# Where eight float32r operands of a mixture-of-experts stage lie in SBUF

## What is computed

```python
x = layernorm(x + ssm(x))
x = layernorm(x + int8_expert(x, fside, ctx))
# mixture: h = x as [1024, 256]; gate_up_proj [8, 352, 256]; down_proj [8, 256, 176]; router_w [8, 256]
probs = softmax(h @ router_w.T); vals, idx = top_k(probs, 2); vals /= vals.sum(-1)
combine[token, idx] = vals
for gup, dp, cw in experts:
    gate, up = split(h @ gup.T, 2)
    out += cw[:, None] * (silu(gate) * up @ dp.T)
x = layernorm(x + out)
```

## The kernel before

| tensors | start modulo 512 |
|---|---|
| `x2_hi`, `x2_lo` (moving in gate_up) | 352 |
| `gu_hi`, `gu_lo` (stationary in gate_up) | 224 |
| `hid_hi`, `hid_lo` (stationary in down) | 416 |
| `dp_hi`, `dp_lo` (moving in down) | 352 |
| `ident`, `ones` | 352 |
| `tokens`, `u_feat`, `w_feat`, `cw1`, `cw2`, `diag` | 128 |
| `gu_raw`; `xq`, `wq`, `scale_rows` | 160; 32 |

## Time and profile before

### The profile page before, as it was taken

One profiled execution on the slowest core, in us unless ns is written; L12 is line 12 of the kernel. 1 busy time (PEld: TensorE's weight loads), 2 busy tenths in 40 slices (PEclk: granted clock), 3 DMA queues, 4 the chain that ended last, 5 costly groups with the idle time before them and its releaser, 6 DMA issues.

```text
span 160.5 us, 3397 instructions
## 1 busy us (share of the span) xinstructions
PE 146.4 (91%) x1158; PEld 139.7 (87%) x1158; DVE 111.2 (69%) x385; ACT 86.9 (54%) x187; POOL 81.0 (50%) x131
## 2 busy tenths in 40 slices
PE   6778579987899999999999999999999999999980
PEld 6566457876799998999999999999999999999970
DVE  3999957989888979699827886966735652444252
ACT  6431496489876787735466866355554404335210
POOL 5613499486966468622119564224835213337421
PEclk9999987999999999999999999999999999999998
DMA  3899990000000374000246100017430025620001
GB/s 104 263 383 422 354 325 22 0 0 0 6 0 4 87 150 121 7 0 4 66 154 146 35 0 33 6 30 158 135 111 0 0 55 122 159 62 6 33 0 65
DMA packets 13313, 14.55 MB, mean 91 GB/s; under 512 B 1744, under 2 KB 13040, under 8 KB 13040
## 3 DMA queue, kind: packets, MB, share of 16 engines
q1 hardware_dynamic: 13296, 14.34, 29.7%
HBM read 13.25 MB, written 1.08 MB: 89 GB/s over the span
## 4 chain that ended last, share of the span: by engine, by line
PE 75%; DMA 7%; DVE 6%; ACT 3%; SPq 3%; issue 2%; POOL 1%; POOLq 0%; ACTq 0%
PE ps_gu L351 13%; PE ps_gu L356 13%; PE ps_gu L352 13%; DMA gu_raw<-in_guT 7%; PE ps_out L372 6%; PE ps_out L376 6%; PE ps_out L373 6%; PE ps_ab L385 3%; PE ps_ab L390 2%; PE ps_s L385 2%; ACT gu_hi L775 1%; PE ps_gu L407 1%; PE ps_ab L486 1%; SPq L255 1%; PE ps_tr L322 1%
## 5 line engine op out<-in xcount | busy, mean ns | idle before, releaser
L351 PE MATMUL ps_gu<-x_hi,gu_hi 128*128 128x256 f32 x176 | 46.5, 286 | 0.0
L352 PE MATMUL ps_gu<-x_hi,gu_lo 128*128 128x256 f32 x176 | 45.6, 281 | 0.0
L1185 POOL TENSOR_TENSOR gu_raw<-gu_raw 128x512 f32<-128x512 f32 (+1 forms) x24 | 28.5, 1196 | 22.2 <-DVE gu_raw L1575 14.8
L356 PE MATMUL ps_gu<-x_lo,gu_hi 128*128 128x256 f32 x176 | 35.2, 282 | 0.0
L351 PEld LDWEIGHTS ps_gu<-x_hi,gu_hi 128*128 128x128 f32 x176 | 33.1, 188 | 0.1
L352 PEld LDWEIGHTS ps_gu<-x_hi,gu_lo 128*128 128x128 f32 x176 | 33.2, 188 | 0.0
L356 PEld LDWEIGHTS ps_gu<-x_lo,gu_hi 128*128 128x128 f32 x176 | 27.0, 188 | 0.0
L1581 DVE TENSOR_TENSOR hid_lo<-gu_raw,hid_hi 128x512 fp32r<-128x512 f32 (+1 forms) x24 | 15.0, 636 | 13.8 <-ACT hid_hi L811 13.8
L811 ACT ACTIVATE hid_hi<-gu_raw 128x512 fp32r<-128x512 f32 (+1 forms) x24 | 14.2, 594 | 13.0 <-POOL gu_raw L1185 12.8
L372 PE MATMUL ps_out<-dp_hi,hid_hi 128*128 128x256 f32 x77 | 20.4, 286 | 0.0
L1575 DVE TENSOR_TENSOR gu_raw<-sil,ps_gu 128x512 f32<-128x512 f32 (+1 forms) x24 | 15.2, 636 | 6.8 <-PE ps_gu L356 4.6
(11 more groups left out here) (271 smaller groups left out, 309.0 us busy)
## 6 DMA issues: line engine op xcount, KB each, us to landing
gu_raw<-in_guT SPq DMA_DIRECT2D x1, 2824.0 KB, 12.0
gu_raw<-share_rows SPq DMA_DIRECT2D x16, 128.0 KB, 3.2
dp_raw<-in_dpT SPq DMA_DIRECT2D x1, 1408.0 KB, 15.3
u_feat<-in_xT SPq DMA_DIRECT2D x4, 256.0 KB, 4.1
w_feat<-in_wT SPq DMA_DIRECT2D x4, 256.0 KB, 9.7
out<-u_feat SPq DMA_DIRECT2D x8, 128.0 KB, 2.0
gu_raw<-share_rows SPq DMA_DIRECT2D x8, 112.0 KB, 2.9
gu_raw<-share_rows SPq DMA_DIRECT2D x8, 96.0 KB, 2.9
```

The source lines that it names most:

```text
L351: pe.matmul(dst, gu_hi[:, c, kind, col], x2_hi[:, b % 2, c], start=(c == 0), stop=False)
L352: pe.matmul(dst, gu_lo[:, c, kind, col], x2_hi[:, b % 2, c], start=False, stop=False)
L356: last = pe.matmul(dst, gu_hi[:, c, kind, col], x2_lo[:, b % 2, c], start=False, stop=(c == DC - 1))
L1185: pool.tensor_tensor(hid[:, lo:hi], hid[:, lo:hi], shares[:, lo:hi], ALU.mult).then_inc(hid_ready, 1)
```

## The change

Eleven tensors are declared ahead of all others: first a filler `lead` of 96 floats (384 bytes, which with the 128 make the next start a multiple of 512), then the eight float32r operands, then `ident` and `ones`. The eight sizes (4,096, 22,528 and 11,264 bytes) are multiples of 512, as are those of `ident` and `ones`, so all ten start at 0 modulo 512. `tokens` through `diag` then start at 0 as well, `gu_raw` at 32, and what follows keeps its order and ends 384 bytes later, with 64 bytes of SBUF left. No instruction is added, removed or moved; `lead` is neither written nor read.

```diff
         ps_moe = [[ps_out[:, 0:D]] * TT] * (B - 1) + [[ps_out[:, 0:D], ps_a[:, 0:D]]]
 
+        sb("lead", [P, 96])
+        x2_hi, x2_lo = sb("x2_hi", [P, 2, DC, S], F32R), sb("x2_lo", [P, 2, DC, S], F32R)
+        gu_hi, gu_lo = sb("gu_hi", [P, DC, 2, EH], F32R), sb("gu_lo", [P, DC, 2, EH], F32R)
+        dp_hi, dp_lo = sb("dp_hi", [P, HC, D], F32R), sb("dp_lo", [P, HC, D], F32R)
+        hid_hi, hid_lo = sb("hid_hi", [P, HC, S], F32R), sb("hid_lo", [P, HC, S], F32R)
+        ident, ones = sb("ident", [P, P]), sb("ones", [P, P])
         tokens = sb("tokens", [P, B, TT, D])
...
         gu_raw = sb("gu_raw", [P, DC, GUW])
-        gu_hi, gu_lo = sb("gu_hi", [P, DC, 2, EH], F32R), sb("gu_lo", [P, DC, 2, EH], F32R)
-
         router_w = sb("router_w", [P, DC, 2 * E], F32R)
         dp_raw = sb("dp_raw", [P, HC, D])
-        dp_hi, dp_lo = sb("dp_hi", [P, HC, D], F32R), sb("dp_lo", [P, HC, D], F32R)
-        ident, ones = sb("ident", [P, P]), sb("ones", [P, P])
...
         st2, mv2, rs2 = sb("st2", [P, TT, 6]), sb("mv2", [P, TT, 2]), sb("rs2", [P, 4, TT])
-
-        x2_hi, x2_lo = sb("x2_hi", [P, 2, DC, S], F32R), sb("x2_lo", [P, 2, DC, S], F32R)
...
-        hid_hi, hid_lo = sb("hid_hi", [P, HC, S], F32R), sb("hid_lo", [P, HC, S], F32R)
```

## The result

The changed kernel takes 163.62 us (162.68 to 164.99, 5 runs) against 160.91 us before: ratio 1.0147, 95% interval 1.0097 to 1.0197. Run again later, 12 runs on another occasion, it gave 1.0104 (1.0070 to 1.0138). (The ratio comes from the single runs. The quotient of the two medians, 1.0168, lies inside its interval.) The changed kernel is slower by 1.0 to 1.5%, where 1.9% less was forecast.

What follows compares the result with a forecast made beforehand. TensorE was taken to bound the kernel: a span of 160.5 us, less 3.2 for cheaper steps, plus 0.1 for lost cover, gave 157.4; with 0.4 from span to median, 157.8 us. The range was 154.8 to 161.5 us.

Steps and rivals of the forecast that it cites:

- What bounds the kernel: From first `gate_up` to last `down`, TensorE goes at its own rate; each nanosecond in 792 matmuls counts at the end.
- That starts matter: In `gate_up` and `down`, putting all eight operands at remainder 0 changes TensorE's step; the forecast's mechanism had chance 0.54.
- The direction: `gate_up` and `down` steps fall to between 110 and 118.6 ns, saving 3.2 us together; faster had chance 0.53.
- the pairs whose two operands start at the same remainder show no excess at all: `ones` with `ones` at 111 ns and `diag` with `u_feat` at 112 ns, taken as nearest in placement.
- the slower rival: Equal starts make load and moving operand collide: `gate_up` and `down` at 124.0 ns, 5.3 us more, 166.2 us; chance 0.16.
- the 113.2 ns put into the sum: `down`'s cheap step, taken for all `gate_up` and `down`: saves 2.85 us in `gate_up`, 0.39 us in `down`.
- nothing happens: How a stream starts, not addresses, decides `down`'s two steps; time stays at 160.9 us; chance 0.30.
- the signs written down ahead, the last: If `down`'s step rises while `gate_up`'s falls, the difference of the two starts counts, and 0 isn't the best.
- The covers named: Slack hiding TensorE's waits, 0.66 us at `gate_up(0, 3, 0)`, 0.15 at the last `hid_lo`; 0.1 us loss taken, 0.6 at most.
- The bound of 0.6 us for loads: Moved load destinations, such as `gu_raw`, were priced at nothing, with 0.6 us as bound on either side.
- The sign given for a mispriced load: If the first `gate_up` moves from its start at 43 us, the loads were mispriced.
- The 0.4 us taken between span and time: The profiled span was put 0.4 us under the runs' median, turning 157.4 us of span into 157.8 us.

Runs made afterwards that it cites:

- e4: The kernel before with `hid_hi` and `hid_lo` moved by 192 bytes, so difference 0 in `down` alone and 128 in `gate_up` as before: ratio 1.0086.
- e6: The changed kernel once more, unaltered, 12 runs on another occasion: ratio 1.0104 to the kernel before.
- e3: The kernel before with `x2_hi` and `x2_lo` moved by 128 bytes, so difference 0 in `gate_up` alone and 192 in `down` as before: ratio 1.0009.
- e2: The kernel before with `x2_hi` and `x2_lo` moved by 64 bytes, so difference 192 in `gate_up` as in `down`: ratio 0.9965.
- e7: The changed kernel with fillers that make the difference 192 in `gate_up` and `down`, `ident` and all behind it unmoved: ratio 0.9923 to the kernel before.
- e5: The changed kernel with fillers giving the eight operands their old remainders, `ident` and all behind it unmoved: ratio 0.9963 to the kernel before.
- map_starts: Block left out: 256 streams of 16 float32r matmuls, one per pair of operand starts in 32-byte steps; means by difference from 116.1 to 119.9 ns.
- map_fine: Block left out: 256 streams of 16 float32r matmuls, difference of starts 0 to 252 bytes in steps of 4; 113.3 to 124 ns a matmul.
- map_entry: Block left out: streams of 24 matmuls at difference 192, entered from other differences or after transposes; after transposes, 23 of 32 were cheap.

## Why the prediction was wrong

**What bounds the kernel: right.** TensorE's step in 792 matmuls sets the stretch; of the others only VectorE's busy time moved, by 0.4 us. e4 and e6, 1.1 and 1.8 us of steps more, came out at 0.86% and 1.04%, which is 1.4 and 1.7 us.

**That starts matter: right.** With nothing changed modulo 256 but the starts of `x2_hi` and `x2_lo`, `gate_up` went from 118.5 to 119.6 ns (e3) and to 116.5 (e2). The timeline has a load of 128x128 and a stream of 256 columns in each step of a dense float32r stretch, and the step is 1.8 to 7.2 ns longer than the 111.4 of the load alone: 113.2 in the earlier trace rows, 118.6 in the earlier trace rows. The load alone goes at one price at both starts tried: the router's loads in the changed kernel, now from 0, step by (97.39 - 96.60) / 7 = 112.9 ns where the earlier trace rows has 111.4, the same within the rounding of the rows.

```profile
96.60 0.19 PEld L320 LDWEIGHTS ps_tr<-router_w,x_hi 128*128 128x128 f32 x1
...
97.39 0.19 PEld L321 LDWEIGHTS ps_tr<-router_w,x_lo 128*128 128x128 f32 x1
```

What makes the excess was not shown: the runs give the length of a step and not what goes on inside it.

**The direction: wrong, and this is the step that failed.** The text took "the pairs whose two operands start at the same remainder show no excess at all" as the nearest row in placement. Those pairs were float32. `ones` with `ones` still goes at 111 ns in the changed kernel, (0.83 - 0.275) / 5:

```profile
30.05 0.83 PE L530 MATMUL ps_tr<-ones 128*128 128x128 f32 x6
```

and float32r pairs with equal starts are at 119.7, the second dearest of the eight differences. A price had been carried from one type of stream to another that isn't alike in the trace either. Both have a load of 128x128, but these float32 records stream 128 columns in their 111 ns and the float32r ones 256 in 113 to 120; two float32 records of 256 columns (line 439, at 65.95 us in the kernel before) take 0.44 us, 220 ns each. The text itself wrote that none of the dense float32r streams in the trace had equal starts, and let that count only for the slower rival. It should have stopped the argument there, and the 113.2 ns put into the sum for all 792 matmuls with it: with differences of 128 and 192 as the only two points measured, the trace couldn't say what 0 costs, and the sign was open. No run shows equal starts at the 113.2 ns that `down` has in its cheap state; in its place the changed kernel showed 119.9 in `gate_up` and 119.8 in `down`.

**The rival that happened** was the slower one, at 0.16. What it went by, sameness of the starts, is half right, and a collision of load and stream was not shown: equal starts are dear (119.7 ns), but a difference of 96 is as dear (119.9), and 20, 84, 132 and 244 are dearer (122 to 124 ns). Its size was too large: it added today's excess once more and had 124.0 ns and 166.2 us; measured were 119.9 ns and 163.6 us. Of the 1.8 us that the steps grew, `gate_up` holds 0.7 and `down` 1.15, about 1.0 of the latter in the 155 steps that had been cheap (155 x 6.4 ns). The text counted on that state for everything, and it was what was lost.

**The other case, "nothing happens",** rested on `down` having two prices at one start. Both are true: the difference decides which prices there are (113.3 and 117.8 ns at 192, 119.3 to 120.0 at 0), and how the stream is entered weighs on which of them it gets (cheap in four of four tries from 0, in none from 224). Of the signs written down ahead, the last drew the right conclusion (the difference counts, and 0 isn't the best) from a case that didn't come: both steps rose.

**Waits, loads and small tensors.** The covers named weren't put to the test, as the stream got no faster. The one of 0.15 us at the last `hid_lo` did give out in e7, where TensorE really was earlier. The bound of 0.6 us for loads was wide enough: e5 shows no loss there. The sign given for a mispriced load, a first `gate_up` that moves from 43 us, can't serve: with the loads where they were before, that start lies at 42.1 us in e2 and e3. The 0.4 us taken between span and time was wrong: within one execution it is 1.7 to 1.8; it didn't matter to the ratio.

## What to carry to other kernels

Where float32r matmuls stand back to back on the critical path, take the step from start to start, and look at the start of the moving operand less that of the stationary one, modulo 256 bytes: here 0 and 96 cost 120 ns, 192 cost 113 to 118, and aligning everything to a round number gave 120 everywhere. A filler of a few dozen bytes moves it (64 bytes in e2, from 118.5 to 116.5 ns), and a small kernel with nothing but such streams maps the price in one run, before any placement is argued for. Don't carry a price from float32 or bf16 matmuls to float32r ones: here 111 ns for 128 columns of float32 and 110 for 256 of bf16 stood beside 113 to 124 for 256 of float32r.

## What the runs showed of the hardware that was not expected

- The step of a dense float32r stream (128 stationary columns, 256 moving) in map_starts and map_fine depends on the difference of the two start addresses modulo 256 bytes, from 113.3 to about 124 ns, and it changes in steps as small as 4 bytes.
- At a difference of 192 (and once at 64) the same code has two steady prices, 113.3 and 117.7 ns (map_starts, map_fine, map_entry); a stream settles in one within its first seven steps or so and keeps it, for 52 of 53 steps in the last stream of `down` before.
- The same float32r matmuls cost 120 ns (difference 0) or 113 ns (192, in its cheap state) by where their two operands start. Whether the load or the stream is held up, and where, no run shows.
